# Attention with a window on one core: maxima as pairs of 64-query products, k kept resident with key 0 in gaps, query 0 computed in the projection

## What is computed

```python
x = x + _L0_attn_ref(_layernorm(x, axis=-1), Wq, Wk, Wv, Wo)
x = x + _L0_ffn_ref(_layernorm(x, axis=-1), fast_b, w_fc, w_proj, u, v, gate)
# attention: H = 16 heads of HD = 16, WINDOW = 128, N_GLOBAL = 1
attend = (dist <= WINDOW) | glb[:, None] | glb[None, :]
logits = where(attend, einsum('bhqd,bhkd->bhqk', q, k) / sqrt(HD), -inf)
out = einsum('bhqk,bhkd->bhqd', softmax(logits), v)
# feed: bitlinear products with ternary weights, r = relu(h), bitlinear(r * r, w_proj)
```

## Time and profile before

| | us |
|---|---|
| runs, median (lowest to highest) | 1385.11 (1384.3 to 1389.28) |
| profiled execution: span, time | 1385.3, 1385.3 |
| PE busy | 1241.6 (90%) |
| DVE busy | 1057.3 (76%) |
| ACT busy | 801.1 (58%) |
| POOL busy | 777.9 (56%) |

### The profile page before, as it was taken

How to read it: one execution, slowest core, us unless ns; L and a number is a source line. 1 busy time by engine, 2 the same in 40 slices (tenths; PEclk the granted TensorE clock), 3 DMA queues, 4 the chain that set the end, 5 groups by cost and what they waited for, 6 DMA issues and landing times. The chain is left out here.

```text
span 1385.3 us, 34119 instructions
## 1 busy us (share of the span) xinstructions
PE 1241.6 (90%) x10205; PEld 827.8 (60%) x10205; DVE 1057.3 (76%) x3288; ACT 801.1 (58%) x1404; POOL 777.9 (56%) x1337
## 2 busy tenths in 40 slices
PE   5999939999999989999899999745799999999997
PEld 4888814445444444444444445322688888888886
DVE  6999758888888878888788888262667767677674
ACT  4778805666766757666577676611345445454454
POOL 1445564777777767777677778820134334334343
PEclk9999957999999999999999999968799999999999
DMA  3999999656687556875468753385212112121100
GB/s 123 333 337 331 309 197 151 104 113 122 117 140 137 102 109 118 137 137 104 105 117 141 137 104 86 138 288 175 91 47 90 48 48 88 45 82 54 45 32 31
DMA packets 174564, 180.61 MB, mean 130 GB/s; under 512 B 24612, under 2 KB 169016, under 8 KB 173368
## 3 DMA queue, kind: packets, MB, share of 16 engines
q1 hardware_dynamic: 174392, 178.57, 54.0%
HBM read 118.47 MB, written 59.25 MB: 128 GB/s over the span
## 5 line engine op out<-in xcount | busy, mean ns | idle before, releaser
L923 DVE CUSTOM_DVE_ANT_0 a_masked<-a_turn,a_band 128x385 f32<-128x385 f32 (+1 forms) x1024 | 512.1, 539 | 91.3 <-PE a_turn L789 72.3
L873 ACT ACTIVATE a_weights<-a_score 128x1024 f32<-128x1024 f32 x384 | 391.8, 1025 | 133.6 <-PE a_score L807 132.1
L682 POOL TENSOR_SCALAR_AFFINE_SELECT a_weights<-a_weights 128x256 f32<-128x256 f32 (+1 forms) x768 | 351.2, 496 | 122.1 <-ACT a_weights L873 122.1
L1338 POOL TENSOR_TENSOR f_square<-f_relu 128x512 f32<-128x512 f32 x128 | 150.9, 1183 | 313.7 <-ACT f_relu L1434 312.8
L830 PE MATMUL a_sum<-a_weights,a_v 128*17 128x384 f32 (+2 forms) x2816 | 228.8, 399 | 3.4 <-POOL a_weights L682 3.3
L1434 ACT ACTIVATE f_relu<-f_bank 128x512 f32<-128x512 f32 x128 | 76.7, 599 | 186.5 <-PE f_bank L200 183.4
L786 PE MATMUL a_turn<-a_k,a_q 96*128 96x384 bf16 (+1 forms) x512 | 165.6, 328 | 11.8 <-issue 6.6
L1466 DVE TENSOR_TENSOR f_square_lo<-f_square,f_square_hi 128x512 fp32r<-128x512 f32 x128 | 106.4, 842 | 89.1 <-POOL f_square L1338 89.1
L1410 PE MATMUL f_bank<-w_w_t,f_square_hi 128*128 128x256 f32 x512 | 133.2, 293 | 16.4 <-DVE f_square_lo L1466 15.1
L807 PE MATMUL a_score<-a_q,a_k 99*128 99x384 bf16 (+2 forms) x704 | 129.1, 275 | 3.0 <-ACT a_weights L873 3.0
L279 POOL TENSOR_TENSOR p_parts<-p_rest,p_parts 128x512 bf16<-128x512 f32 x64 | 74.1, 1169 | 97.8 <-ACT p_parts L342 97.8
(11 more groups left out here) (184 smaller groups left out, 2592.1 us busy)
## 6 DMA issues: line engine op xcount, KB each, us to landing
qk_parts<-p_parts SPq DMA_DIRECT2D x64, 384.0 KB, 3.2
a_q<-qk_parts SPq DMA_DIRECT2D x48, 192.0 KB, 5.0
a_q<-qk_parts SPq DMA_DIRECT2D x144, 64.0 KB, 4.8
v_ones<-p_va SPq DMA_DIRECT2D x16, 544.0 KB, 5.0
p_x<-in_x SPq DMA_DIRECT2D x16, 512.0 KB, 6.0
k_whole<-p_kf SPq DMA_DIRECT2D x16, 512.0 KB, 3.7
attention<-a_o SPq DMA_DIRECT2D x16, 512.0 KB, 3.3
f_o<-attention SPq DMA_DIRECT2D x16, 512.0 KB, 4.3
```

Of the source, the lines that this page charges most:

```text
L682: ins = pool.affine_select(out=cut, in_=cut, compare_op=ALU.is_ge, fill=0.0, base=0, pattern=[[0, NQ // 2], [0, m], [sign, P]], channel_mu ...
L873: act.activation(pe_w[:, us.upar, c * CHUNK:(c + 1) * CHUNK], score[c % 2][:], ACT.Exp).then_inc(s_exp, 1)
L923: dve.tensor_tensor_reduce(out=masked[:, j, first:3 * P + 1], in0=bank[:, lo:hi + 1], in1=band[:, lo:hi + 1], scale=1.0, scalar=NEG, op0=A ...
L1338: pool.tensor_tensor(r2[:, j % 4, :], r[:, j % 4, :], r[:, j % 4, :], ALU.mult).then_inc(s_sq, 1)
```

## The change

It has these parts.

1. Maxima: a tile of 128 queries is two products of 64 stationary columns with 322 keys each (320, with the gap columns between blocks), into the two halves of the bank's partitions. The order of tiles is by query block first. `turn` banks, M, S, scores and sums have a new order (`AFTER_TILE`), M has 16 stationary columns.
2. k of a sequence stays in SBUF (`kt`), in blocks of 129 columns whose first is key 0, so the product with one column and the copy of key 0 go. The projection writes k in this form. Each block is loaded once.
3. Cutting the band: `SCORE_TILES` places the blocks so that each third block is cut alike, four selects a unit instead of twelve.
4. Lags are `L_MAX, L_SHIFT, L_SCORE, L_SUM, L_OUT = 2, 3, 4, 5, 6`. The rest and LOW part of the maxima move from POOL to DVE, LOW ahead of tile 12.
5. Query 0: its q comes from a norm of four rows at the start of the projection; folded with Wk into 16 more columns for each sequence beside v's 256, it makes its logits with v. v takes one bank for each block of 128 tokens, two banks in turn. Maxima, exponential and sums of row zero stand at the end of the projection. `kf` is not made. `stage_row_zero` becomes `stage_weights`, without row zero.
6. q and k parts are stored by part (12 stores of 128 KB and up for a group instead of four), and laid out so that a unit's load is contiguous.

```diff
+KPITCH = P + 1
+KGT = TB * KPITCH
+KROW = T // P * KPITCH
+HALF = P // 2
+WINDOW = 5 * HALF + 2
...
+            pe.wait_ge(s_x0v, 12)
+            for k in range(KT):
+                for m in range(KT):
+                    ins = pe.matmul(c_bank[:, k * B * H:(k + 1) * B * H], w_in[:, 1, m, k * P:k * P + P],
+                                    q0_d[:, m].rearrange("p b h -> p (b h)"), start=(m == 0), stop=(m == KT - 1))
+            ins.then_inc(s_x0pe, 1)
...
-                    for c in range(2):
-                        wait(pe, s_vout, (q.g - 1) * 2 + c + 1)
-                        for t in range(2):
-                            cut = slice((2 * c + t) * P, (2 * c + t + 1) * P)
-                            ins = three_pass(pe, v_bank[c][:, t * D:t * D + D], [a[:, cut] for a in xh],
-                                             [a[:, cut] for a in xl], [wt_hi[:, 2, k, :] for k in range(KT)],
-                                             [wt_lo[:, 2, k, :] for k in range(KT)])
-                        ins.then_inc(s_v, 1)
+                    for t in range(TB):
+                        wait(pe, s_vout, q.g * TB + t - 1)
+                        cut = slice(t * P, (t + 1) * P)
+                        three_pass(pe, v_bank[t % 2][:, 0:D + H], [a[:, cut] for a in xh], [a[:, cut] for a in xl],
+                                   wv(wv_hi, q), wv(wv_lo, q)).then_inc(s_v, 1)
...
+            pe.wait_ge(s_rv, 1)
+            pe.transpose(turn_bank[0:B * H, 0:P], m_tok[:], ident[:]).then_inc(s_rpe, 1)
+            pe.wait_ge(s_rv, 3)
+            pe.matmul(over_bank[:, 0:B * H], ones[0:B * H, :], m_diag[:], start=True, stop=True).then_inc(s_rpe, 1)
+            pe.wait_ge(s_rexp, 1)
+            for n in range(NB):
+                for b in range(B):
+                    ins = pe.matmul(sum_bank[QR * b:QR * b + H, 0:VROW], w0[:, b, n, :], v_of[:, b, n, 0:VROW],
+                                    start=(n == 0), stop=(n == NB - 1))
+            ins.then_inc(s_rpe, 1)
...
-                        if u >= KT:
-                            act.activation(kf[:, q.par, u - KT, :], qk_bank[u][:], ACT.Copy)
-                        act.activation(parts[:, q.par, u, PLACE[u // KT][HIGH], :], qk_bank[u][:], ACT.Copy,
+                        act.activation(part_of(q, u, HIGH), blocks(qk_bank[u]), ACT.Copy,
                                        scale=QSCALE if u < KT else 1.0).then_inc(s_high, 1)
...
-                    for c in range(2):
-                        act.wait_ge(s_v, q.g * 2 + c + 1)
-                        for t in range(2):
-                            ins = act.activation(va[:, q.par, 2 * c + t, :, 0:HD],
-                                                 v_bank[c][:, t * D:t * D + D].rearrange("p (h e) -> p h e", h=H),
-                                                 ACT.Copy)
-                        ins.then_inc(s_vout, 1)
+                    for t in range(TB):
+                        act.wait_ge(s_v, q.g * TB + t + 1)
+                        act.activation(va[:, bass.ds(q.g * TB + t, 1), :].rearrange("p a (h e) -> p (a h) e", e=VW)
+                                       [:, :, 0:HD],
+                                       v_bank[t % 2][:, 0:D + H].rearrange("p (h e) -> p h e", e=HD),
+                                       ACT.Copy).then_inc(s_vout, 1)
...
+            for b in range(B):
+                ins = dve.tensor_tensor(wv_lo[:, b, :, 0:D], banks[2][:].rearrange("p (k n) -> p k n", k=KT),
+                                        wv_hi[:, b, :, 0:D].bitcast(F32), ALU.subtract)
+            ins.then_inc(s_wlo, 1)
+            dve.wait_ge(s_chi, 1)
+            dve.tensor_tensor(wv_lo[:, :, :, D:D + H],
+                              c_bank[:, 0:KT * B * H].rearrange("p (k b h) -> p b k h", k=KT, b=B),
+                              wv_hi[:, :, :, D:D + H].bitcast(F32), ALU.subtract).then_inc(s_clo, 1)
...
-SCORE_TILES = ((0, 0, 1, 0, 3), (0, 3, -1, 0, 1),
+SCORE_TILES = ((0, 0, 1, 0, 3), (0, 3, 4, 3, 1),
                (1, 0, 0, 0, 2), (1, 2, 3, 2, 2),
-               (2, 0, 4, 3, 1), (2, 1, 2, 1, 3))
+               (2, 0, -1, 0, 1), (2, 1, 2, 1, 3))
 HEAD_COLS = 3 * GT
-CUT_LOW = ((0, 1), (6, 1), (8, 2))
-CUT_HIGH = ((2, 2), (5, 1), (11, 1))
-SUM_ORDER = (1, 2, 0, 3, -1, 4)
+CUT_AHEAD, CUT_BEHIND, CUT_STEP = 0, 2, 3
+SUM_ORDER = (1, -1, 2, 4, 0, 3)
 CHUNK = 2 * GT
 CHUNKS = NQ * HEAD_COLS // CHUNK
 TILES = NQ * TB
-TURN_OF_M, TURN_OF_S, TURN_BANKS = 3, TILES + 1, 3
-TURN_OF_TILE = tuple(j if j < TURN_OF_M else j + 1 for j in range(TILES))
+TURN_OF_M, TURN_OF_S, TURN_BANKS = 2, 6, 3
+TURN_OF_TILE = tuple(j + (j >= TURN_OF_M) + (j >= TURN_OF_S - 1) for j in range(TILES))
 TILE_OF_TURN = {k: j for j, k in enumerate(TURN_OF_TILE)}
 TURNS = TILES + 2
 assert TURNS % TURN_BANKS == 0
-L_KEY0, L_MAX, L_SHIFT, L_SCORE, L_SUM, L_OUT, L_STORE = 2, 3, 4, 6, 7, 8, 9
+MASKED = (TB - 1) * KPITCH + WINDOW
+L_MAX, L_SHIFT, L_SCORE, L_SUM, L_OUT = 2, 3, 4, 5, 6
 AFTER_TILE = (
-    (("score", 0), ("score", 1)), (("score", 2),), (("score", 3), ("M", 0)), (("score", 4), ("score", 5)),
-    (("sum", 0),), (("score", 6),), (("score", 7),), (("sum", 1),),
-    (("score", 8),), (("score", 9),), (("sum", 2),), (("score", 10),),
-    (("score", 11),), (("sum", 3),), (("sum", 4),), (("sum", 5), ("S", 0)))
+    (("score", 0), ("score", 1)), (("M", 0),), (("score", 2),), (("score", 3),),
+    (("S", 0),), (("score", 4), ("score", 5)), (("sum", 0),), (("score", 6),),
+    (("sum", 1), ("sum", 2)), (("score", 7),), (("score", 8),), (("sum", 3),),
+    (("score", 9),), (("score", 10),), (("score", 11),), (("sum", 4), ("sum", 5)))
...
-                        rows_of = qk_dram[which, h0 * HD:(h0 + NQ) * HD, :, tokens]
-                        sp.dma_start(buf[0:3 * HD, :, cols], rows_of.rearrange("(h d) s t -> (d s) h t", d=HD)
-                                     ).then_inc(s_load[u.gpar][u.hq], DMA)
...
+                    places = [(1, k_dram[bass.ds(u.batch * GB + c, 1), u.hq], kt[u.hq][:, :, c * KGT:(c + 1) * KGT])
+                              for c in CHUNKS_OF[u.gi]]
+                    places += [(0, q_dram[bass.ds(u.g, 1), u.hq], qw[u.gpar][u.hq])]
+                    for which, src, dst in places:
+                        src = src.rearrange("a d s h t -> (a d) s h t")
+                        sp.dma_start(dst[0:PARTS * HD], src.rearrange("d s h t -> (d s) h t")).then_inc(landed, DMA)
...
-                    sp.wait_ge(s_shift, u.n * 3 + 3)
+                    sp.wait_ge(s_shift, u.n + 1)
                     for part in range(SHIFT_ROWS):
                         row = qw[u.gpar][u.hq][SLOT_ROWS + part:SLOT_ROWS + part + 1, :, :]
                         sp.dma_start(row.rearrange("s h (t q) -> s (h t) q", q=P),
                                      shift[:, u.upar, part, :]).then_inc(s_row[u.upar], DMA)
...
-                w = pe_w[:, u.upar].rearrange("p (h c q) -> p h c q", h=NQ, q=P)
-                for runs, sign in ((CUT_LOW, 1), (CUT_HIGH, -1)):
-                    for c, m in runs:
-                        cut = w[:, half * NQ // 2:(half + 1) * NQ // 2, c:c + m, :]
-                        ins = pool.affine_select(out=cut, in_=cut, compare_op=ALU.is_ge, fill=0.0, base=0,
-                                                 pattern=[[0, NQ // 2], [0, m], [sign, P]],
-                                                 channel_multiplier=-sign)
+                w = pe_w[:, u.upar].rearrange("p (a c q) -> p a c q", a=2, q=P)
+                for first, sign in ((CUT_AHEAD, 1), (CUT_BEHIND, -1)):
+                    cut = w[:, half, first::CUT_STEP, :]
+                    ins = pool.affine_select(out=cut, in_=cut, compare_op=ALU.is_ge, fill=0.0, base=0,
+                                             pattern=[[0, NQ // 2 * HEAD_COLS // P // CUT_STEP], [sign, P]],
+                                             channel_multiplier=-sign)
...
-                    lo = P if ux.gi == 0 and t == 0 else 0
-                    hi = 2 * P if ux.gi == GB - 1 and t == TB - 1 else 3 * P
-                    q, kk = qw[ux.gpar][ux.hq], kw[ux.gpar][ux.hq]
-                    lhs = q[0:SLOT_ROWS, h, t * P:t * P + P]
-                    pe.matmul(turn[k % TURN_BANKS][:, lo:hi], lhs, kk[0:SLOT_ROWS, h, t * P + lo:t * P + hi],
-                              start=True, stop=True)
-                    key = ux.hq * NQ + h
-                    pe.matmul(turn[k % TURN_BANKS][:, hi:hi + 1], lhs, k0[0:SLOT_ROWS, key:key + 1],
-                              start=True, stop=True).then_inc(s_tile, 1)
+                        pe.wait_ge(s_load[ux.gpar][ux.hq], loaded(ux))
+                    bank_read(TURN_OF_TILE[j])
+                    t, h = divmod(j, NQ)
+                    for half in range(2):
+                        start, lo, hi = keys_of(ux.gi, t, half)
+                        q0 = t * P + half * HALF
+                        ins = pe.matmul(turn[TURN_OF_TILE[j] % TURN_BANKS][half * HALF:(half + 1) * HALF, lo:hi],
```

(19 more changed lines are left out.)

682 lines of the change are left out of this document (364 added, 318 removed).

## The result

Slower: 1582.32 us median (1566.19 to 1588.36) against 1384.7 us (1383.51 to 1389.28) of the kernel before on the same chip, a ratio of 1.1398 with a 95% interval of 1.1335 to 1.1461. The forecast was 1498 us, range 1395 to 1550. The direction was right, the time is 32 us above the range. Three of the kernels further down (e3_split, e9_one_column, e12_split_less) ran at very different granted clocks from one run to the next, so they have no ratio, their fastest run is named beside the median with its mean clock, and their traces are of slower runs than that.

What follows compares the result with a forecast made beforehand. PE's instruction stream was taken to set attention's time. From 1385.3 us: attention +95, projection groups +25, prologue +7.5, projection end +9, weights -24, giving 1498 us, range 1395 to 1550.

Steps and rivals of the forecast that it cites:

- TensorE's speed: Attention: units priced from the old steady stretch, where the clock share is 0.99; no term for added time at lower clock.
- The drains: Attention on PE: 20 more changes of column grouping a unit, each emptying the array, at 0.095 us: +1.9 us a unit.
- Rival A: Attention: 64 columns beside 128 cost no change, but the shift rows' wait becomes 1.1 us; 1410 us, chance 0.13.
- B: Attention: 64 columns beside 128 cost no change and the shift rows no wait; unit 9.8 us, 1345 us, chance 0.15.
- The pair: Maxima tiles: two 64-column halves run together, 0.17 us against 0.19 a tile, -0.3 us a unit.
- rival C: Maxima tiles: the two halves run one after the other, +2.1 us a unit, 1626 us, chance 0.05.
- PE's sum: Attention: PE's instruction stream for one unit, 10.16 us before and 11.95 us after, including 0.1 us of remaining waits.
- The shift rows: Attention: PE waits for the shift rows' DMAs before the next unit's first score, 0.45 us a unit (0 to 1).
- DVE and POOL: Attention: masked maximum 490 ns on DVE, saving used up by moved shift work; band cuts 1.07 us on POOL, saving hidden.
- Projection: Projection stage: +25 us for groups waiting on v's banks, +7.5 us prologue, +9 us row zero's serial work at the end.
- Rival D: Projection: the v wait does not bind because ACT is ahead of its order, -25 us; no separate chance given.
- Weights: Weights stage after attention: row zero's work goes, so feed starts earlier, -24 us (-20 to -26).

Runs made afterwards that it cites:

- e3_split: Kernel before the change, with each tile's 384-column product and the one-column product beside it both made as two 64-query products: 1692.76 us.
- e9_one_column: Kernel before the change, with only the one-column product of key 0 made as two 64-query products: 1799.21 us.
- e12_split_less: Kernel before the change, with only each tile's 384-column product made as two 64-query products: 2024.95 us.
- e2_whole: Changed kernel with each tile of maxima again one product of 128 queries, with 386 columns: 1523.63 us.
- e8_low_whole: Changed kernel with LOW made ahead of tile 8 and each tile of maxima one product of 128 queries and 386 columns: 1471.07 us.
- e4_vfirst: Changed kernel with ScalarE's copies of the first two v blocks ahead of the last middle part in the projection: 1562.19 us.
- e1_lag: Changed kernel with one more lag step between the shift rows' transfer and the unit's first score product: 1499.62 us.

## Why the prediction was right or wrong

- **TensorE's speed: the step that failed.** The sum priced every unit at full clock, and put the time at the lower level, beyond what the kernel before has, at nothing. It named the 0.58 of the start and 0.99 of the steady stretch, and then took 0.99 along into a program with another rhythm. The 24 intervals that hold time at the lower clock are together 66 us longer than 12.1 each, of which 7 are the back edges' wait for issue that was there before. Attention is 66 us over its forecast: 57 of these lie in the intervals (833.1 against 665.8 + 110), where the time at the lower clock is more than the whole excess, as a plain unit is shorter than forecast; the other 9 lie at the two ends, 7 of them in the tail, which shrank by 8 us and not by 15. The other 15 of the 81 us between 1497.8 and the span are the projection's 14 and the weights' 1. Without the 66 us at the lower clock the time would have been some 1516 us, inside the range. Shown by three kinds of run: the fill in the wait (faster with more work, the drains unchanged), the two runs with early rows (0.97), and, with the rival named there, the drains in the old kernel (mean clock 0.69 to 0.90 in the fastest runs, 0.50 for 730 us and more in the traces).
- **The drains: right.** 0.10 us for each change at 64 columns, forecast 0.095, and 12.1 for a plain unit, forecast 12.3 to 12.4 with the wait. Rival A, that 64 columns beside 128 cost nothing, is refuted, and B with it. The Trainium skill's rule ("TensorEngine Tiling (Array Packing)", section "Key Properties") that changing the mode drains TensorE agrees with these rows. It speaks of a drain, not of the clock behind it.
- **The pair: right.** Side by side; rival C is refuted. PE's sum was 11.6, not 11.95.
- **The shift rows: place right, size and kind off.** The wait is 44.3 us over 57 units, 0.78 each, within 0 to 1 but not 0.45. The sum held the wait as a price of its own beside PE's work. The wait grows as that work shrinks, which only rival A priced (1.1 us): with PE at 11.6 and the ring at some 12, less work on PE gains little (e2_whole: 11.8 a unit, waits of 60.9 us instead of 36.1).
- **DVE and POOL: right.** 489 ns for a masked maximum (forecast 490), 1092 ns for a cut (1.07 us). DVE came next in line once PE and the rows were freed (41.4 us of waits for its maxima in e8_low_whole), which the sum, with PE as the bound, didn't price.
- **Projection: +55.5 against +41.5.** Groups: plain ones at some 11.5 (forecast 11.2), +29.6 with two dips of the clock, at the top of 15 to 30. Rival D is refuted by e4_vfirst. Prologue +9.8 (5 to 10). Tail +16.1, just past 5 to 15: row zero's sums are 4.8 of the 7 missing. Some 6 of their 10.3 us lie at the lower clock (0.28 x 11 / 0.5), which by an estimate at half speed is about 3 of the 4.8; the rest is the sums' own size.
- **Weights: right**, -23 against -24.

The account of the 82 us between the changed kernel and e1_lag: 44 of waits, and 85 us less at the lower clock in the long windows. What a microsecond there costs is estimated from the two ends of e3_split's runs: (1 - 0.897) x 1554 / 0.5 = 320 us at the lower level in 1556, 762 in 1742, so 186 us for 442, 0.42 each. 44 + 36 = 80, which closes to 2 us. The two windows don't cover the same units: e1_lag starts attention with 61 us at the lower level, the changed kernel with 55, so by whole intervals the difference is nearer 72 us than 85, and the sum 74 of 82. How the rest divides stays open.

Open: why the old kernel with its tiles split falls so much further than the changed one. e3_split has 32 changes a unit, as many as e1_lag, and is at 0.50 for long stretches where e1_lag is at 0.97; with 38, e12_split_less never leaves 0.50. So the number of changes alone doesn't set the clock. No run here separates the length of the pair, the one-column products, the count of products and the kernels' other differences.
